# Tiles of 128 edges, two and three near tiles, and an older layout of PSUM banks and degree sums, in a four-layer graph network kernel

## What is computed

```
# l0: edge-conditioned convolution, then batch norm and relu
h1 = relu(edge_attr_16 @ W1 + b1);  w = (h1 @ W2 + b2).reshape(-1, 16, 16)
out = segment_sum(einsum('ei,eio->eo', x[src], w), dst) + x @ root + bias
# l1: tensor product; gathers by dst, sums by src
m = silu(einsum('ei,ej,ijh->eh', x[dst], edge_attr_8, W_msg_tp) / sqrt(128))
agg = segment_sum(m, src) @ W_msg_lin / 4
x = x + h + silu(einsum('ni,nh,ihk->nk', h, agg, W_upd_tp) / 16) @ W_upd_lin / 4
# l2a, l2b: relational convolution, twice, then log_softmax
norm = 1 / max(cnt[dst, edge_type], 1)
out_i = sum over edges of (x[src] @ W[edge_type]) * norm + x @ root + bias
# l3: x / sqrt(out_degree) gathered by src, summed by dst, / sqrt(in_degree)
```

## Time and profile before

| | us |
|---|---|
| median of 2 runs (4581.88 and 4586.84) | 4584.36 |
| the profiled execution's own time | 4555.6 |
| its span, first to last instruction | 4553.4 |
| PE busy in it | 4339.6 (95%) |
| DVE | 4121.4 (91%) |
| POOL | 3284.9 (72%) |
| ACT | 3235.6 (71%) |

### The profile page before, as it was taken

How to read it: one execution, slowest core, us unless ns; L and a number is a source line. 1 busy time by engine, 2 the same in 40 slices (tenths; PEclk the granted TensorE clock), 3 DMA queues, 4 the chain that set the end, 5 groups by cost and what they waited for, 6 DMA issues and landing times.

```text
span 4553.4 us, 107759 instructions
## 1 busy us (share of the span) xinstructions
PE 4339.6 (95%) x30477; PEld 3261.8 (72%) x30477; DVE 4121.4 (91%) x11864; ACT 3235.6 (71%) x5359; POOL 3284.9 (72%) x2515
## 2 busy tenths in 40 slices
PE   4999999999997999999979999998999999799998
PEld 3777777777775777777747777776777777566665
DVE  5999999999997999999969999997999998888887
ACT  3777777777774777777737777775777777677776
POOL 4888888888883777777727777775777775688886
PEclk8999999999998999999989999999999999899999
DMA  3111111111111222222211111111111111111111
GB/s 72 21 17 18 17 18 17 18 18 18 18 17 40 61 59 61 59 60 60 59 37 27 27 28 27 27 28 39 27 28 28 26 28 23 30 31 31 30 31 24
DMA packets 336556, 148.67 MB, mean 33 GB/s; under 512 B 250040, under 2 KB 322532, under 8 KB 336392
## 3 DMA queue, kind: packets, MB, share of 16 engines
q0 software_dynamic: 104000, 59.31, 10.1%
q1 hardware_dynamic: 232517, 88.88, 7.8%
HBM read 135.45 MB, written 9.80 MB: 32 GB/s over the span
## 4 chain that ended last, share of the span: by engine, by line
PE 81%; DVE 10%; issue 5%; ACT 2%; DMA 1%; SPq 1%; DVEq 0%; POOL 0%; POOLq 0%; ACTq 0%
PE acc L600 37%; PE rows_ps L757 16%; PE rows_ps L693 7%; PE bank L773 5%; PE bank L693 4%; PE counts L607 3%; PE eaT_ps L765 3%; DVE raw L1258 2%; PE rows_ps L681 2%; DVE stationary L1234 2%; PE eaT_ps L669 1%; DVE one_hot L1206 1%; PE counts L604 1%; DVE rows_ps L1321 1%; ACT stack L928 1%
## 5 line engine op out<-in xcount | busy, mean ns | idle before, releaser
L600 PE MATMUL acc<-one_hot,stationary 125*128 125x392 bf16 x12000 | 2335.4, 329 | 39.5 <-DVE stationary L1234 35.1
L584 POOL DMA_INDIRECT gathered<-table_l,row_numbers x1200 | 1607.3, 1339 | 461.1 <-issue 349.1
L600 PEld LDWEIGHTS acc<-one_hot,stationary 125*128 125x128 bf16 x12000 | 1157.3, 100 | 709.0 <-DVE stationary L1234 49.9
L866 ACT ACTIVATE distances<-count_hi,fields 125x392 bf16<-125x392 f16 (+1 forms) x2500 | 1227.5, 560 | 0.0
L1234 DVE TENSOR_TENSOR stationary<-mask,parts 125x1024 bf16<-125x1024 bf16 x1500 | 943.3, 683 | 0.3 <-ACT mask L851 0.2
L851 ACT CAST mask<-is_lo 125x1024 bf16<-125x1024 f32 x500 | 523.1, 1046 | 447.3 <-DVE is_lo L1187 393.5
L584 POOL DMA_INDIRECT fields_all<-table_l,row_numbers x500 | 646.3, 1293 | 259.6 <-issue 114.8
L1206 DVE TENSOR_SCALAR one_hot<-count_hi,fields 125x392 bf16<-125x392 f16 x2300 | 734.4, 341 | 13.5 <-issue 13.5
L1321 DVE COPY_PREDICATED rows_ps<-near_bits_now,rows_ps 125x320 f32<-125x320 int8 (+3 forms) x1600 | 579.7, 362 | 162.6 <-PE rows_ps L757 118.6
L584 POOL DMA_INDIRECT gathered<-table_l2a,row_numbers x400 | 512.7, 1282 | 282.6 <-DVE parts L1216 119.4
L757 PE MATMUL rows_ps<-node_parts,h1T 125*125 125x192 bf16 (+1 forms) x7200 | 678.3, 252 | 27.0 <-DVE node_parts L1285 19.6
(11 more groups left out here) (213 smaller groups left out, 4706.6 us busy)
## 6 DMA issues: line engine op xcount, KB each, us to landing
near_key<-near_keys_by_chunk SPq DMA_DIRECT2D x300, 122.1 KB
gathered<-table_l,row_numbers POOLq DMA_INDIRECT x1200, 2.8
fields<-edge_fields SPq DMA_DIRECT2D x500, 31.2 KB
near_key<-near_keys_by_chunk SPq DMA_DIRECT2D x100, 91.6 KB
fields_all<-table_l,row_numbers POOLq DMA_INDIRECT x500, 3.5
gathered<-table_l2a,row_numbers POOLq DMA_INDIRECT x400
gathered<-table_l2b,row_numbers POOLq DMA_INDIRECT x400
ea<-in_edge_attr SPq DMA_DIRECT2D x100, 62.5 KB
```

Source lines behind the costliest of these rows:

```text
L584: pool.indirect_dma_start(out=gathered[ph][:, s, t, :], in_=table[ph], out_offset=None, in_offset=bass.IndirectOffsetOnAxis(ap=row_numbers ...
L600: mm = pe.matmul(acc[:, :], stationary[:, s, k, t, :, :].rearrange("p a b -> p (a b)"), one_hot[:, s, t, :], start=first and t == 0 and k ...
L866: ins = act.activation(distances[:, i * n:(i + 1) * n], count_hi[:, 0:n], ACT.Abs, scale=-1.0, bias=fields[:, s, k, t:t + 1].bitcast(F32))
```

## The change

`EP` becomes 128 and there are 98 chunks of 1024 edge places, 352 more than edges. Partition 127 has fewer edges: the first `WHOLE` = 54 chunks are full (128 rows), the other 44 have 127 rows, and padding values stand in the last one. Every load of edge data is therefore made from one of two views, of 128 or of 127 rows, and loads over all chunks (src, dst, types, `near_ea8`) are cut in two. SP's loops are cut at chunk 54. Four memsets on DVE set the padding, and SP starts behind them.

l1 has 2 near tiles and l2a, l2b 3, so that POOL gathers 6 and 5 tiles per chunk; l3 stays at 4, l0 at 8.

`rows_ps` has two banks, and the transposed outer products go to bank 2. In l1 the counts matmul has `lo_bf` as stationary operand, the mask of 8 columns in bf16 that ACT copies, and gives 8 x 392 results. l1's fold by three additions becomes one strided `tensor_reduce`. Node rows of l1 hold counts instead of inverse counts; for near tiles DVE picks the edge's count and takes its maximum with 1 and its reciprocal, in small instructions behind the outer product, three of them with a wait for the one before.

```diff
-EP, T = 125, 8
+EP, T = 128, 8
-TILES = E // EP
-CHUNKS = TILES // T
+CHUNKS = -(-E // (EP * T))
+TILES = CHUNKS * T
-NEAR_OF = {"l0": (0, 0), "l1": (3, 3), "l2a": (4, 4), "l2b": (4, 4), "l3": (4, 4)}
+LAST_EP = EP - 1
+WHOLE = (E - LAST_EP * TILES) // T
+WHOLE_EDGES = EP * WHOLE * T
+NEAR_OF = {"l0": (0, 0), "l1": (2, 2), "l2a": (3, 3), "l2b": (3, 3), "l3": (4, 4)}
...
-        rows_ps = ctx.enter_context(nc.psum_tensor("rows_ps", [128, 3, 512], F32))
-        turned_ps = eaT_ps[:].rearrange("p t e -> p (t e)").bitcast(F32)
+        rows_ps = ctx.enter_context(nc.psum_tensor("rows_ps", [128, 2, 512], F32))
+        TURNED_BANK, MESSAGE_BANK = 2, (4, 3)
...
+        def by_rows(v):
+            names = "(p c t) f -> p c t f" if len(v.shape) == 2 else "(p c t) -> p c t"
+            return (v[0:WHOLE_EDGES].rearrange(names, p=EP, t=T), v[WHOLE_EDGES:].rearrange(names, p=LAST_EP, t=T))
...
-            sp.wait_ge(ev("x_cleared"), 1)
+            sp.wait_ge(ev("x_cleared"), 5)
-            sp.dma_start(src[:], A["src"].rearrange("(p t) -> p t", p=EP)).then_inc(ev("edges_in"), 16)
+            for into, k in ((src, "src"), (dst, "dst"), (typ, "edge_type_8")):
+                whole, ragged = by_rows(A[k])
+                sp.dma_start(into[:, 0:WHOLE * T], whole.rearrange("p c t -> p (c t)")).then_inc(ev("edges_in"), 16)
+                sp.dma_start(into[0:LAST_EP, WHOLE * T:], ragged.rearrange("p c t -> p (c t)")).then_inc(ev("edges_in"), 16)
...
+            def rows_of(views, chunk, ragged):
+                view, at = (views[1], chunk - WHOLE) if ragged else (views[0], chunk)
+                return view[:, bass.ds(at, 1), :].rearrange("p c n -> p (c n)")
...
-                            sp.dma_start(near_ea8[:], ea8_d[:, :, (T - NEAR1) * RELATIONS:]).then_inc(ev("diagonals_in"), 16)
                             sp.wait_ge(ev("near_keys_turned"), 1)
                             sp.dma_start(near_key_d, near_key_rows[:]).then_inc(ev("near_keys_stored"), 16)
                             sp.wait_ge(ev("diagonals_cleared"), len(bd) - 2)
+                            for views, rows, chunks in ((ea8_d[0], EP, slice(0, WHOLE)), (ea8_d[1], LAST_EP, slice(WHOLE, CHUNKS))):
+                                sp.dma_start(near_ea8[0:rows, chunks, :], views[:, :, (T - NEAR1) * RELATIONS:]
+                                             ).then_inc(ev("diagonals_in"), 16)
                         later_copies(chunk - 2)
...
-                        mm = pe.matmul(counts[:, :], mask[:, s, t, :, :].rearrange("p a b -> p (a b)"), one_hot[:, s, t, :],
+                        mm = pe.matmul(counts[0:LO, :], lo_bf[:, s, t, :], one_hot[:, s, t, :],
...
+                    act.copy(lo_bf[:, s], is_lo[:, s])
...
-                if ph == "l2a" or ph == "l2b":
+                if ph != "l3":
                     near_types(ph, chunk, s)
...
-                    dve.tensor_copy(near_inverse[:, s, 0:count], rows[:, :, 0, F:ROW1])
+                    dve.tensor_tensor(near_is_type[:, 0:count], near_is_type[:, 0:count], rows[:, :, 0, F:ROW1],
+                                      ALU.mult).then_inc(near_counted, 1)
...
+                if ph == "l1":
+                    dve.wait_ge(near_counted, 3 * chunk + 1)
+                    dve.tensor_reduce(near_count[:], near_is_type[:, 0:count], AX.X, ALU.add).then_inc(near_counted, 1)
+                    dve.wait_ge(near_counted, 3 * chunk + 2)
+                    dve.tensor_scalar(near_count[:], near_count[:], 1.0, None, ALU.max).then_inc(near_counted, 1)
+                    dve.wait_ge(near_counted, 3 * chunk + 3)
+                    dve.reciprocal(edge_norm[:, bass.ds(chunk * T + far("l1", s), NEAR1)], near_count[:])
...
-                fold(4).then_inc(ev("l1_products"), 1)
-                fold(2).then_inc(ev("l1_products"), 1)
-                st.mark(dve.tensor_tensor(raw[:, s, 0:n], products[:, :, 0, :], products[:, :, 1, :], ALU.add))
+                dve.wait_ge(ev("l1_products"), chunk + 1)
+                st.mark(dve.tensor_reduce(raw[:, s, 0:far("l1", s)], product1[:, 0:far("l1", s)].rearrange("p t (j h) -> p t h j", h=F), AX.X, ALU.add))
```

## The result

| kernel | us | runs |
|---|---|---|
| before | 4584.36 (4581.88 to 4586.84) | 2 |
| changed | 5571.30 (5560.56 to 5582.03) | 2 |

The ratio is 1.215, 95% interval 1.205 to 1.226: slower, by 987 us where the prediction had 176. The profiled execution took 5582.03 us, its span 5580.2. The two runs of each kernel lie within 0.4% of one another, so this isn't a slow run beside a fast one.

What follows compares the result with a forecast made beforehand. After the change POOL's gathers, one per far tile, were to pace the kernel. l0 -26.6, l1 +89.8, l2 +97.6, l3 -12.9 and start +30 made +178 on 4555.6 us; with 28.8 carried over, 4760 us, range 4710 to 4820.

Steps and rivals of the forecast that it cites:

- The step that failed first: POOL's gathers: 128 rows taken to cost the same as 125, 1.205 us at the shortest; upper bound 80 us in all.
- the prediction's own last sign of being wrong: The prediction is wrong if gathers of 128 rows have another shortest time than 1.205 us.
- SP's loads: Edge loads of 127 rows: by the divisor rule they run on one engine, where 125 rows use five.
- The POOL-bound terms: One more gather per chunk: l1 at 9.58 us per chunk, +89.8 us; l2a and l2b at 7.93, +97.6 together.
- the 0.5 us per chunk: l1: time gathers wait beside DVE's work, added to their floor of 9.07 us; 0.37 taken for l2.
- the rule named for it: A GpSimd DMA whose descriptors are to be written waits for the whole of a VectorE instruction in a 2-port mode.
- Rival B: Gathers don't set the pace; DVE paces l1 at 8.9 us per chunk, PE l2 at 6.6: 4435 us. Chance 0.04.
- DVE in l1: DVE's work per chunk: 2.06 us out, 2.49 in, so 8.47 us busy and 8.9 with gaps, under 9.58.
- The counts matmul with an 8-column stationary: PE in l1: same 392 columns, so the same time; no cost.
- The start: Before the chunks run steadily: +30 us, from edges landing at 31 us, faster field stores and SP blocked 51 us.
- rival A: The 127-row loads spread over engines as the 125-row ones do: 4714 us. Chance 0.17.
- E (PE's clock): PE, waiting some 2 us per chunk in l1, runs half its work there at 1.2 GHz: +150, 4910 us. Chance 0.04.

Runs made afterwards that it cites:

- e8: Changed kernel with fewer rows per gather: eight sizes from 128 to 96 in l0, 128, 113, 100 and 64 in l3; 5167 us.
- e5: The changed kernel once more, not altered, on another chip; 4439 us, beside 4556 for the kernel before.
- e3: Kernel before (tiles of 125 edges) with two near tiles in l1 and three in l2a and l2b, nothing else; 4803 us.
- e1: Changed kernel with tiles of 125 edges again and every load from one view; 4777 us.
- e16: Changed kernel with the 128-column mask in the counts matmul and l1's fold by three additions, both as before; 4391 us.
- e11: Changed kernel with gathers of 128, 125, 112, 125 and 120 rows in l0, l1, l2a, l2b and l3; 5206 us.
- e12: Kernel before with gathers of 112, 125, 120, 112 and 96 rows in l0, l1, l2a, l2b and l3; 5175 us.
- e17: Kernel before with gathers of 25, 125, 25, 16 and 112 rows in l0, l1, l2a, l2b and l3, on chip 10; 5646 us.
- e15: Kernel before with gathers of 25, 125, 25, 16 and 112 rows in l0, l1, l2a, l2b and l3, on chip 1; 4519 us.

## Why the prediction was wrong, point by point

**The step that failed first** is "whether a gather of 128 rows costs more than one of 125 no row shows; bounds are nothing and 3/125". The bound below nothing was left out, by the argument that a time with a floor doesn't fall with more rows. It falls from 1.205 to 0.94 us, as e8's divisor rule has it: 128 rows are shared by 16 engines and 125 by 5. This was the prediction's own last sign of being wrong, "another shortest time than 1.205 us". I had used this very rule, with its consequence for 127 rows, for SP's loads two paragraphs on, and not for POOL's gathers. A gather with its gap is then 0.94 + 0.30 = 1.24 us, and 6 of them 7.4 us, less than l1 needs anyway (8.15 with the mean of 1.058 in l1 of e5).

**The POOL-bound terms** were right in mechanism and size for the gathers they assumed: e3 has 9.59 and 7.96 us per chunk where I had 9.58 and 7.93, and the 0.5 us per chunk for what a gather waits beside DVE's work was right with them. They don't apply at 128 rows. (782.7 less 734.1 is 48.6 and not 48.8, which changes nothing.) That the gather of 1.97 us "agrees" with the rule named for it is more than the row carries: it ran beside two TENSOR_TENSORs of DVE, and no row shows one of them in a 2-port mode, while gathers beside TENSOR_SCALARs of the near one-hots took 0.94 us in e5 (4002.44). That a gather waits beside some of DVE's work is shown, by which rule isn't.

**Rival B**, at 0.04, is what happens where nothing slows: "it decides if a gather with its gap takes under 1.41 us". It gave 4435, and e5 took 4439. That they are so near is luck: B changes the first measurement's 4584 by -149 us, and e5 is 117 below the 4556 of its own chip. l1 took 934/98 = 9.53 us per chunk against 8.9, +62 us, and the rest was some 30 us shorter than B had. Of these 14 are l3's, which fell to 616/98 = 6.29 us from 6.43, because POOL had been its pace.

**DVE in l1** was put at 8.47 us busy and is 870/98 = 8.88; the strided reduction was right (1.438 us against 1.44, by its group in e5). Most of the miss lies in the one-hots. Those of 392 columns, which I left as they were, take 377 ns against 315 before, three per chunk, +0.19 us. Those of the near tiles, two per chunk, I had 0.12 us shorter each; they take 383 ns against 335, +0.33 in all. e1, with tiles of 125 edges and the same steps, has 321 and 282, and e16, without the strided reduction, 316 and 382; what makes them longer no run isolates. "The counts matmul with an 8-column stationary has the same 392 columns, hence the same time" is wrong too. Rows of the waits of e5, whole run:

```profile
PEld counts L637 <- issue: 254.6, 784, 0.6
```

That is 0.32 us of PEld's idle time ahead of each narrow load; in l1 PE is busy 9.18 us per chunk (899.63/98) with it and 7.97 (780.78/98) without. It costs next to nothing in time (4439 against 4435), as DVE sets l1's pace: cover that would be gone with a faster DVE.

**The start** was forecast at +30. Chunk 3's first gather is at 134 us (e5: 130) against 102.5 before: +27 to +32, right as a sum. Pieces of the chain of the changed kernel:

```profile
21.66 14.81 DMA stage<-in_edge_type
...
87.52 40.64 SPq L437
```

The edges landed at 36.5, not 31 (before 21.4), and SP is blocked for 40.6 us instead of 51 (before 21.58). The 127-row loads are as slow as few engines make them, so rival A falls; the two sizes were each off, and offset each other.

**What none of the cases had**, and what made 4439 into 5571, is the rest, about 1130 us: the late signals and the stops. The prediction put nothing for a wait that no engine's work explains. Of my rivals E (PE's clock) is the nearest, and is a follower here: the granted clock is 0.93 in the mean against 0.983, and PE falls to the lower of its levels, 1.2 GHz, after stops, as it did after a wait in the earlier trace rows: behind a stop of 4.89 us at 4985.83 in the chain, the stretch 4992.5 to 4999.5 is granted 0.53. But in l3 of the first measurement the clock is 0.97 and the stage 164 us longer than e5's. The clock alone doesn't carry that.

**What is shown and what isn't.** Shown: the same program takes 4439 on one chip and 5404 on another, with the kernel before at 4556 and 4557; stages with gathers of 125 rows stay as they were on slowing chips, in both tile sizes (e11's l1 949 as in e1; e12's l1 846 and e17's 854 against 849 before); l0, l2 and l3 with gathers near 0.94 us lose 100 to 470 us there and l1 38 to 180, whatever the engines, the rows and the tile size (unspaced); e8's l0, where gathers of 1.2 to 2.6 us stand among the short ones, loses nothing, but its l3, mixed too, loses 129 (745 against 616). In l3 and in e17's l2a the late signals arrive within 2 us of the end of a row of gathers. Not shown: what holds back PE's next instruction and PE's signal, whether it is the chip or the time of the measurement, and where the border lies. The cause of the 1130 us stays open.

## What to carry to other kernels

Before a tile size is chosen, factor it: in the gathers measured here the largest divisor up to 16 of their rows set the time, so that 128 rows took less than 125, and 127 more than twice either. A step that makes an engine's instructions shorter can be worth less than nothing where it exposes a limit that the old pace hid, and this limit was there on some chips and not on others; a gain from such a step is to be measured on several chips, beside the old kernel. Here tiles of 128 edges with the other kernel's counts and folds took 4345 us (0.954) on one chip and 5426 and 5397 on two others, so the kernel before is the one to keep unless the chip is known.

## What the runs showed of the hardware that I had not expected

- A gather's time on POOL by its rows: 0.92 us (64 and 96), 0.96 (112), 0.99 (120), 1.01 (100), 1.20 (125), 1.29 (124), 2.36 (113), 2.6 (127), and 0.94 for 25 rows (e15).
- PE took one 392-column matmul every 0.72 us for four in a row (5006.92 to 5009.09) without a wait that the profile shows, where 19 take 3.33 us in the earlier trace rows; its signal reached DVE some 5 us late, 1.2 to 2 us behind the last of a row of POOL's short gathers. Such stages were on four of the seven numbered chips, and none of them had gathers of 125 rows.
- Ahead of a stationary operand of 8 columns between ones of 128, PE's loading stands idle for 0.32 us each time (784 times in e5), with the same moving operand.
- Loading a near one-hot of 128 columns takes 99 ns in e5 (mean), 125 columns took 138 before. The Trainium skill, TensorE: Matmul & The Clock Gate (section "Weight-path perf modes — Fast Weight Load (FWL) and DoubleRow"), states that the fast load is for 128 weights of a type other than FP32; both rows agree.
